# VectorE adds a chunk's window sums one step later, and GpSimd waits for seven gathers ahead of the eighth

## The chip, the cores and the metric

The kernel runs on one core of one Trainium2 chip. Its time is the device time of one execution in microseconds (us); where a kernel is timed, the median of its runs is given. The engines are TensorE (PE in the rows; its weight loads PEld), VectorE (DVE), ScalarE (ACT), GpSimd (POOL) and SyncE (SP). Each engine works through its own list of instructions in order, and they meet only through semaphores. DMAs are issued here by SP and by GpSimd.

## The reference, cut to what matters

A graph-attention layer over 6250 nodes and 200000 edges, and after it a layer of experts. The change lies in the edges of the first.

```python
h_fwd = h @ W_forward.T
h_rev = h @ W_reverse.T
messages = h_fwd[src] * direction[:, 0:1] + h_rev[src] * direction[:, 1:2]   # 200000 x 64
scores = leaky_relu(einsum('ef,hf->eh', messages, attn), 0.2)                # 4 heads
exp_scores = exp(scores - scores.max(axis=0))
sum_exp = segment_sum(exp_scores, dst)
norm = exp_scores / (sum_exp[dst] + 1e-10)
outs = [segment_sum(messages * norm[:, hd:hd + 1], dst) for hd in range(4)]
```

## The kernel before

First a table with one row of 136 numbers for each node is made (both products and their scores). Then comes the edge loop, which is what the change touches: the edges, sorted by destination, are taken in 98 chunks of 2048 (16 sets of 128). The loop is written with two chunks in its body, one for each of the two halves of the row buffer `rows` (`RING` = 2, slot `s`); the first two and the last four chunks are written out beside it. After it the nodes are normalised and routed, and the experts run.

A chunk's table rows come in two ways. Fourteen sets of 128 rows (`KG`) are gathered by GpSimd, one indirect DMA each (line 262). Two sets (`FILL`) are made without a DMA: VectorE builds two 0/1 matrices from the source numbers (`build_hot`, line 1043, tile `onehot`), TensorE multiplies each with the table that it holds in SBUF (`fetch`, line 966, 28 matmuls into `p_hot`), and VectorE picks the row out of seven candidates (`keep`, lines 1053 and 1058). The last two chunks gather all of their sets.

In step c VectorE does the following: it weighs the rows with the edges' weights (lines 990, 993, 996), makes the 0/1 matrix of destinations `hot` (1002), scores and their running maximum (1008, 1010, 1015), the messages `msg` (1019), and `hot_ex`, the destinations times the exponentials from ScalarE (1023). Then it keeps the two sets of chunk c+1 that TensorE has fetched, builds the first 0/1 matrix of chunk c+2, adds chunk c's eight windows of sums from PSUM into the accumulator (`finish`, line 985, tile `shared`), and builds the second 0/1 matrix of chunk c+2. In step c TensorE fetches the second set of chunk c+1, sums chunk c's messages into the eight windows (`sum_units`, line 878, tile `p_win`, semaphore `summed`), and fetches the first set of chunk c+2.

GpSimd runs ahead by one chunk. For chunk c it waits ahead of the first gather for the messages of chunk c-2 (whose buffer half it fills), ahead of the second for the sums of chunk c-2 (`summed`), ahead of the eighth for the scores of chunk c-1, and ahead of the twelfth for the messages of chunk c-1. `settle` is an increment that has nobody waiting for it. Each gather counts 16 on `gathered[s]` when it has landed; VectorE waits for the whole count of the chunk at the start of step c (`all_rows`). SP loads each chunk's indices with its edge weights, and the source numbers `key` for the 0/1 matrices, each repeated for all partitions.

Of the kernel before, what the change touches and what calls it, by code (L numbers as in the profile page):

```python
# [51 lines left out]
NCH = -(-EDGES // (CHUNK * RING)) * RING  # L52
# [10 lines left out]
KG = K - FILL  # L63
# [38 lines left out]
def after(eng, sem, count):  # L102

    if isinstance(count, int) and count <= 0:
        return
    eng.wait_ge(sem, count)


def settle(eng, turns):


    eng.sem_inc(turns, 1)
# [107 lines left out]
def stage_edges(nc, tensors, g):  # L220
# [4 lines left out]
    with ExitStack() as edges:  # L225
# [30 lines left out]
        gathered = [esem(f"gathered{s}") for s in range(RING)]  # L256
        prepared = esem("edges_prepared")

        def gather(pool, s, ks, done):

            for k in ks:
                pool.indirect_dma_start(out=rows[:, s, k, :], out_offset=None, in_=table,  # L262
                                        in_offset=bass.IndirectOffsetOnAxis(ap=index[:, s, 0, k:k + 1], axis=0))\
                    .then_inc(done, 16)
# [514 lines left out]
        with ExitStack() as ctx:  # L779
# [23 lines left out]
            msg_ready = sem("messages_ready")  # L803
# [5 lines left out]
            summed = sem("window_summed")  # L809
# [7 lines left out]
            def chunks(eng, begin, step, begun=0):  # L817


                loaded = begin(0)  # L820
                for s in range(begun, RING):
                    step(s, s, 0, loaded)
                with eng.Fori(1, NIT - 2) as it:
                    loaded = begin(it)
                    for s in range(RING):
                        step(it * RING + s, s, it, loaded)
                for it in range(NIT - 2, NIT):
                    loaded = begin(it)
                    for s in range(RING):
                        step(it * RING + s, s, it, loaded)  # L830

            def final(c):

                return isinstance(c, int) and c == NCH - 1
# [5 lines left out]
            def whole(it):  # L840

                return isinstance(it, int) and it == NIT - 1
# [9 lines left out]
            def fill_of(s, it):  # L852

                return (it - 1) * HOT + s * FILL

            def coming(s, it, ahead, j):


                t, jt = (s + ahead) % RING, it + (s + ahead) // RING
                if isinstance(jt, int) and not 0 < jt < NIT - 1:  # L860
                    return None
                return fill_of(t, jt) + j, t, jt, j
# [35 lines left out]
            @block.gpsimd  # L898
            def _(pool):
                def step(c, s, it, _):  # L900
                    pool.wait_ge(index_ready[s], 16 * (it + 1))
                    after(pool, msg_ready, c - RING + 1)
                    settle(pool, turns)
                    begun = EARLY_SETS if isinstance(c, int) and c == EARLY else 0
                    sets = K_LAST if final(c) else K if whole(it) else KG

                    def piece(a, b):
                        gather(pool, s, range(max(a, begun), min(b, sets)), gathered[s])

                    piece(0, 1)  # L910
                    after(pool, summed, c - 1)
                    settle(pool, turns)
                    piece(1, 7)
                    pool.wait_ge(score_ready, c)
                    settle(pool, turns)
                    piece(7, 11)
                    pool.wait_ge(msg_ready, c)
                    settle(pool, turns)
                    piece(11, K)
                pool.wait_ge(prepared, 1)  # L920
                chunks(pool, lambda it: None, step, EARLY)
# [53 lines left out]
            def _(dve):  # L975
# [11 lines left out]
                def step(c, s, it, loaded):  # L987
                    all_rows(dve, c, s, it)
                    attr_of = index[:, s, 1:3, :].bitcast(F32)
                    dve.tensor_tensor(rows[:, s, :, 0:COLS], rows[:, s, :, 0:COLS],  # L990
                                      attr_of[:, 0, :].unsqueeze(2).broadcast_to([P, K, COLS]), ALU.mult)\
                       .then_inc(fwd_part, 1)
                    dve.tensor_tensor(p_part[:, :, :], rows[:, s, :, COLS:COLS + HD],  # L993
                                      attr_of[:, 1, :].unsqueeze(2).broadcast_to([P, K, HD]), ALU.mult)\
                       .then_inc(rev_part, 1)
                    dve.tensor_tensor(rev_p, rows[:, s, :, COLS + HD:ROW],
                                      attr_of[:, 1, :].unsqueeze(2).broadcast_to([P, K, HEADS]), ALU.mult)\
                       .then_inc(rev_score, 1)
                    if isinstance(c, int) and c == 0:
                        dve.wait_ge(s_iota, 1)  # L1000
                    after(dve, val_ready, c)
                    dve.tensor_tensor(hot[:, :, :],
                                      dst_rel[:, ds(c * K, K)].unsqueeze(2).broadcast_to([P, K, W]),
                                      iota_p.unsqueeze(1).broadcast_to([P, K, W]), ALU.is_equal)\
                       .then_inc(hot_ready, 1)
                    dve.wait_ge(fwd_part, c + 1)
                    dve.wait_ge(rev_score, c + 1)
                    dve.tensor_tensor(raw[:, :, :], rows[:, s, :, HD:COLS], rev_p, ALU.add).then_inc(raw_ready, 1)
                    dve.wait_ge(raw_ready, c + 1)
                    dve.scalar_tensor_tensor(out=score[:, :, :], in0=raw[:, :, :], scalar=0.2, in1=raw[:, :, :],  # L1010
                                             op0=ALU.mult, op1=ALU.max).then_inc(score_ready, 1)
                    dve.wait_ge(score_ready, c + 1)
                    after(dve, max_taken, c)
                    real = K_LAST if final(c) else K
                    dve.tensor_tensor(run_max[:, 0:real, :], run_max[:, 0:real, :], score[:, 0:real, :], ALU.max)\
                       .then_inc(max_taken, 1)
                    dve.wait_ge(rev_part, c + 1)
                    after(dve, summed, c)
                    dve.tensor_tensor(msg[:, :, 0:HD], rows[:, s, :, 0:HD], p_part[:, :, :], ALU.add)\  # L1019
                       .then_inc(msg_ready, 1)  # L1020
                    dve.wait_ge(hot_ready, c + 1)
                    dve.wait_ge(exp_ready, c + 1)
                    dve.tensor_tensor(  # L1023
                        hot_ex[:, :, :, :],
                        hot[:, :, :].unsqueeze(2).broadcast_to([P, K, HEADS, W]),
                        ex[:, :, :].unsqueeze(3).broadcast_to([P, K, HEADS, W]), ALU.mult)\
                       .then_inc(val_ready, 1)
                    extra_windows(c, s, loaded[s])
                    if coming(s, it, 1, 0):
                        keep(*coming(s, it, 1, 0))  # L1030
                    if coming(s, it, 1, 1):
                        keep(*coming(s, it, 1, 1))
                    if coming(s, it, 2, 0):
                        build_hot(*coming(s, it, 2, 0))
                    finish(c)
                    if coming(s, it, 2, 1):
                        build_hot(*coming(s, it, 2, 1))

                def build_hot(f, s, it, j):

                    dve.wait_ge(key_ready[s], 16 * it)
                    after(dve, hot_rows, f - FILL + 1)
                    dve.tensor_tensor(onehot[:, j, :, :],  # L1043
                                      key[:, s, j, :].unsqueeze(1).broadcast_to([P, GP, P]),
                                      group_p.unsqueeze(2).broadcast_to([P, GP, P]), ALU.is_equal)\
                       .then_inc(hot_built, 1)
# [14 lines left out]
                def finish(c):  # L1061

                    words = load_own(dve, firsts[:, ds(c * UPC, UPC)], NP - 1)
                    dve.wait_ge(summed, c + 1)
                    for u in range(UPC):
                        after(dve, added, c * UPC + u)
                        add_window(p_win[0:MSG, u * HEADS * W:(u + 1) * HEADS * W], words[u])\
                            .then_inc(added, 1)
# [40 lines left out]
                dve.wait_ge(zeroed, 1)  # L1109
                dve.wait_ge(x_zeroed, NPART)  # L1110
                chunks(dve, begin, step)


def stage_nodes(nc, tensors, g):
# [1080 lines left out]
```

## Time and profile before

| | |
|---|---|
| median of 3 timed runs | 2554.95 us (2554.32 to 2557.01) |
| span of the profiled execution | 2909.8 us |
| busy in that span: TensorE, VectorE, GpSimd, ScalarE | 2151.1, 1860.1, 1744.0, 350.5 us |

The page gives the profiled execution's span from its first to its last instruction, and no time of its own beside that; whatever lies around the span comes on top. The span is 354.9 us longer than the median of the timed runs. Durations in the rows are therefore those of one execution that is some 14% longer than those that were timed. "issue" as the releaser of a wait says that the engine waited for nothing that the profile shows, "remote" that the event has no instruction to it in the trace.

### The profile page before, as it was taken

What the parts mean: (1) busy time and instruction counts of PE and PEld (TensorE: products, weight loads), DVE (VectorE), ACT (ScalarE), POOL (GpSimd) and SP (SyncE); (2) the same over time, 40 slices, a digit from 0 to 9 for tenths busy, and PEclk for the clock granted to TensorE, in tenths of its full rate; (3) what the DMA queues carried; (4) which work ended last, traced back from release to release, by engine and by line L of the source; (5) the groups of instructions that cost most, each with busy time, mean ns of one, the idle gap of its engine ahead of it and who ended that gap; (6) DMA issues with size and microseconds to landing.
All of it is one profiled execution on the core that took longest, in us unless ns stands there. A gap on an engine that the chain in (4) does not pass through costs nothing.

```text
span 2909.8 us, 44243 instructions
## 1 busy us (share of the span) xinstructions
PE 2151.1 (74%) x11977; PEld 1813.9 (62%) x11978; DVE 1860.1 (64%) x4481; ACT 350.5 (12%) x936; POOL 1744.0 (60%) x1757
## 2 busy tenths in 40 slices
PE   6587877778877676877777776777763547999990
PEld 6466765666666565666666665566653446888880
DVE  6666666657666665666576666567664566666656
ACT  4000000000000000000000000000002433434444
POOL 6667666667666666666666666567663554333326
PEclk8698888878788898988798988889875558999995
DMA  5222222222222222222222222222224456656657
GB/s 185 54 53 56 50 50 50 52 51 53 50 51 48 50 53 53 50 51 51 50 50 55 53 53 50 49 50 56 50 46 126 136 184 186 205 193 194 198 166 266
DMA packets 176304, 256.65 MB, mean 88 GB/s; under 512 B 47078, under 2 KB 120999, under 8 KB 176004
## 3 DMA queue, kind: packets, MB, share of 16 engines
q0 software_dynamic: 53696, 121.60, 16.9%
q1 hardware_dynamic: 122564, 134.56, 15.2%
q8 instruction: 16, 0.26, 0.0%
q14 instruction: 28, 0.23, 0.0%
HBM read 218.11 MB, written 38.79 MB: 88 GB/s over the span
## 4 chain that ended last, share of the span: by engine, by line
PE 32%; DVE 26%; issue 17%; another core or an unknown queue 14%; DVEq 7%; DMA 2%; POOL 1%; ACT 1%; SPq 0%; ACTq 0%; POOLq 0%
PE p_hot L966 28%; DVE p_hot L1053 4%; DVE onehot L1043 3%; DVEq L1702 3%; DVE shared L985 2%; DVEq L869 2%; DVE p_part L993 2%; DVE hot_ex L1023 1%; PE p_y L1870 1%; DVE p_y L1925 1%; PE p_h L1860 1%; DVE rows L990 1%; PE p_win L878 1%; DVE second L1905 1%
## 5 line engine op out<-in xcount | busy, mean ns | idle before, releaser
L262 POOL DMA_INDIRECT rows<-node_table,index x1375 | 1411.7, 1027 | 742.4 <-issue 446.5
L966 PE MATMUL p_hot<-parts,onehot 128*128 128x476 f32 x5264 | 1379.7, 419 | 467.7 <-DVE onehot L1043 256.0
L966 PEld LDWEIGHTS p_hot<-parts,onehot 128*128 128x128 f32 x5264 | 1092.9, 210 | 725.3 <-issue 283.1
L1053 DVE SCALAR_TENSOR_TENSOR p_hot<-place_no,place_of_source,p_hot 128x476 f32<-128x476 f32 x376 | 250.7, 712 | 350.4 <-remote 291.3
L985 DVE TENSOR_TENSOR shared<-shared,p_win 65x64 f32 x784 | 170.9, 218 | 361.2 <-remote 258.7
L878 PE MATMUL p_win<-hot_ex,msg 128*65 128x64 f32 x3136 | 231.7, 237 | 75.5 <-DVE hot_ex L1023 58.4
L928 ACT ACTIVATE ex<-score,neg_shift 128x64 f32<-128x64 f32 x98 | 34.3, 350 | 2087.2 <-DVE score L1010 1824.7
L878 PEld LDWEIGHTS p_win<-hot_ex,msg 128*65 128x65 f32 x3136 | 226.2, 152 | 94.7 <-issue 86.4
L1711 POOL DMA_INDIRECT expert_rows<-ys,back x104 | 103.1, 992 | 269.3 <-DVE ys L1930 195.5
L1058 DVE TENSOR_REDUCE rows<-p_hot 128x136 f32<-128x952 f32 x188 | 216.0, 1149 | 6.5
L1860 PEld LDWEIGHTS p_h<-xt,shared 128*128 128x128 f32 x1664 | 198.1, 193 | 35.2 <-ACT xt L1802 29.8
L1860 PE MATMUL p_h<-xt,shared 128*128 128x128 f32 x1664 | 210.2, 280 | 9.8 <-ACT xt L1802 7.5
L1870 PE MATMUL p_y<-shared,hid_t 128*128 x832 | 199.2, 383 | 10.4 <-DVE hid_t L1897 9.8
L1043 DVE TENSOR_TENSOR onehot<-key,p_dve 128x896 fp32r<-128x896 f32 x188 | 202.4, 1077 | 0.0
L1870 PEld LDWEIGHTS p_y<-shared,hid_t 128*128 128x128 f32 x832 | 151.0, 192 | 27.9 <-issue 11.2
L1281 POOL DMA_INDIRECT dispatched<-xn,slot_i x98 | 100.7, 1027 | 95.0 <-issue 72.5
L990 DVE TENSOR_TENSOR rows<-rows,index 128x1088 f32<-128x1088 f32 x98 | 126.2, 1287 | 36.1 <-issue 18.1
L1897 DVE TENSOR_SCALAR hid_t<-p_h,shared 128x128 f32<-128x128 f32 x208 | 63.4, 347 | 124.8 <-PE p_y L1870 68.3
L1019 DVE TENSOR_TENSOR msg<-rows,p_part 128x1024 f32<-128x1024 f32 x98 | 119.0, 1214 | 3.1 <-issue 3.1
L1023 DVE TENSOR_TENSOR hot_ex<-hot,ex 128x1024 f32<-128x1024 bf16 x98 | 119.4, 1219 | 1.0 <-issue 0.5
L993 DVE TENSOR_TENSOR p_part<-rows,index 128x1024 f32<-128x1024 f32 x98 | 120.0, 1225 | 0.0
L1833 ACT ACTIVATE own<-xs,is_first 128x256 f32<-128x256 f32 x104 | 52.9, 508 | 207.3 <-DVE is_first L1908 189.9
(268 smaller groups left out, 1401.3 us busy)
## 6 DMA issues: line engine op xcount, KB each, us to landing
shared<-in_w SPq DMA_DIRECT2D x120, 512.0 KB
rows<-node_table,index POOLq DMA_INDIRECT x1375
xs<-dispatched SPq DMA_DIRECT2D x104, 129.5 KB
key<-hot_keys SPq DMA_DIRECT2D x94, 128.0 KB
shared<-expert_rows SPq DMA_DIRECT2D x12, 896.0 KB, 8.6
token_rows<-in_x SPq DMA_DIRECT2D x7, 896.0 KB
shared<-in_x SPq DMA_DIRECT2D x7, 768.0 KB
out<-shared SPq DMA_DIRECT2D x6, 896.0 KB, 7.5
```

Of the source, the lines that this page charges most:

```text
L262: pool.indirect_dma_start(out=rows[:, s, k, :], out_offset=None, in_=table, in_offset=bass.IndirectOffsetOnAxis(ap=index[:, s, 0, k:k + 1] ...
L878: last = pe.matmul(psum[0:MSG, u * HEADS * W:(u + 1) * HEADS * W], msg[:, k, :], weighted[:, k, :, :].rearrange("p h w -> p (h w)"), start ...
L966: last = pe.matmul(p_hot[:, j, d, 0:PLACES * COLS], onehot[:, j, gr, :], parts[:, gr:NT:GP, m, d * COLS:(d + 1) * COLS], start=(gr == 0 an ...
L985: return dve.tensor_tensor(to, to, psum.rearrange("p (h w) -> p h w", h=HEADS), ALU.add)
L990: dve.tensor_tensor(rows[:, s, :, 0:COLS], rows[:, s, :, 0:COLS], attr_of[:, 0, :].unsqueeze(2).broadcast_to([P, K, COLS]), ALU.mult)\
L993: dve.tensor_tensor(p_part[:, :, :], rows[:, s, :, COLS:COLS + HD], attr_of[:, 1, :].unsqueeze(2).broadcast_to([P, K, HD]), ALU.mult)\
L1023: dve.tensor_tensor(hot_ex[:, :, :, :], hot[:, :, :].unsqueeze(2).broadcast_to([P, K, HEADS, W]), ex[:, :, :].unsqueeze(3).broadcast_to([P ...
L1043: dve.tensor_tensor(onehot[:, j, :, :], key[:, s, j, :].unsqueeze(1).broadcast_to([P, GP, P]), group_p.unsqueeze(2).broadcast_to([P, GP, P ...
L1053: last = dve.scalar_tensor_tensor(out=found[:, d], in0=place_no[:, :].unsqueeze(2).broadcast_to([P, PLACES, COLS]), scalar=place[:, ds(f, ...
L1058: dve.tensor_reduce(rows[:, s, KG + j, :].rearrange("p (d c) -> p d c", d=2), found.rearrange("p d v c -> p d c v"), AX.X, ALU.add).then_i ...
L1860: last = pe.matmul(p_h[:, u, f // 2, (f % 2) * P:(f % 2 + 1) * P], w1_r[:, r % R5, c, f * P:(f + 1) * P], xt[:, u, c, :], start=(c == 0), ...
L1870: last = pe.matmul(p_y[:, u, 0:D], hid_t[:, u, c, :], w2_sb[:, ds(e, 1), c, :] .rearrange("p a d -> p (a d)"), start=(c == 0), stop=(c == ...
```

## The change

In VectorE's step the eight window adds (`finish`) of chunk c leave step c and come in step c+1, between the running maximum and the messages; the first 0/1 matrix of chunk c+2 is built ahead of them, in step c. The messages' own wait for `summed` falls away, because the adds that now stand ahead of them wait for the same sums. The last chunk's adds stand behind the loop. A wait for VectorE's own messages of the step before is put ahead of line 993. GpSimd waits ahead of a chunk's eighth gather until the chunk's first seven have landed (`not begun` leaves out chunk 1 alone, whose first eight are gathered ahead of the loop).

```diff
                     piece(1, 7)
+                    if not begun:
+                        pool.wait_ge(gathered[s], 16 * (KG * it + 7))
                     pool.wait_ge(score_ready, c)
                     settle(pool, turns)
                     piece(7, 11)
...
                        .then_inc(fwd_part, 1)
+                    after(dve, msg_ready, c)
                     dve.tensor_tensor(p_part[:, :, :], rows[:, s, :, COLS:COLS + HD],
...
                        .then_inc(max_taken, 1)
+                    if coming(s, it, 2, 0):
+                        build_hot(*coming(s, it, 2, 0))
+                    if not (isinstance(c, int) and c == 0):
+                        finish(c - 1)
                     dve.wait_ge(rev_part, c + 1)
-                    after(dve, summed, c)
                     dve.tensor_tensor(msg[:, :, 0:HD], rows[:, s, :, 0:HD], p_part[:, :, :], ALU.add)\
...
                         keep(*coming(s, it, 1, 1))
-                    if coming(s, it, 2, 0):
-                        build_hot(*coming(s, it, 2, 0))
-                    finish(c)
                     if coming(s, it, 2, 1):
                         build_hot(*coming(s, it, 2, 1))
...
                 chunks(dve, begin, step)
+                finish(NCH - 1)
```

On VectorE, in the loop's body of the kernel before, the end of a step reads as follows: the last pick (`rows<-p_hot`), the first 0/1 matrix, the loading of the eight window places (`firsts`), and the first of the eight adds.

```order
L1058 TENSOR_REDUCE rows<-p_hot 128x136 [waits one_hot_rows_kept]
L1041 ISA
L106 ISA [waits keys_loaded0]
L1043 TENSOR_TENSOR onehot<-key,p_dve 128x896 [waits one_hot_rows_summed]
L869 ISA
L869 TENSOR_LOAD firsts
L985 ISA [waits window_added,window_summed]
L985 TENSOR_TENSOR shared<-shared,p_win 65x4x16
```

In the changed kernel the same instructions stand in the middle of the step, behind the running maximum.

```order
L1018 TENSOR_TENSOR run_max<-run_max,score 128x64 [waits max_taken,score_ready]
L106 REGISTER_ALU [waits keys_loaded1]
L1046 TENSOR_TENSOR onehot<-key,p_dve 128x896 [waits one_hot_rows_summed]
L869 ISA
L869 TENSOR_LOAD firsts
L987 ISA [waits window_added,window_summed]
L987 TENSOR_TENSOR shared<-shared,p_win 65x4x16
```

What moved is the matrix and the adds, from behind the picks to ahead of the messages; the wait for the sums went with the adds and is now for those of the chunk before.

On GpSimd, in the loop's body of the kernel before, one chunk of the second buffer half is this row of gathers (`x5` is five in a row).

```order
L262 DMA rows<-node_table,index 128x136 [waits index_ready1,messages_ready]
L262 DMA rows<-node_table,index 128x136 [waits window_summed]
L262 DMA rows<-node_table,index 128x136 x5
L914 REGISTER_ALU
L262 DMA rows<-node_table,index 128x136 [waits score_ready]
L262 DMA rows<-node_table,index 128x136 x3
L262 DMA rows<-node_table,index 128x136 [waits messages_ready]
L262 DMA rows<-node_table,index 128x136 x2
```

In the changed kernel it is this one.

```order
L262 DMA rows<-node_table,index 128x136 [waits index_ready1,messages_ready]
L262 DMA rows<-node_table,index 128x136 [waits window_summed]
L262 DMA rows<-node_table,index 128x136 x5
L916 REGISTER_ALU [waits gathered1]
L262 DMA rows<-node_table,index 128x136 [waits score_ready]
L262 DMA rows<-node_table,index 128x136 x3
L262 DMA rows<-node_table,index 128x136 [waits messages_ready]
L262 DMA rows<-node_table,index 128x136 x2
```

No gather moved; one wait more stands between the seventh and the eighth, on the count that the gathers themselves raise by landing.

## Rows read from the trace of the kernel before

**Rows 1.** The page, busy time: the span and the number of instructions.

```profile
span 2909.8 us, 44243 instructions
```

**Rows 2.** Stretches: length, engines' busy time (instructions), granted TensorE clock, DMA share, GB/s.

```profile
0.00:62.00 62.00, 43.15 (x322) 40.27 (x323) 37.16 (x154) 27.85 (x63) 42.58 (x45) 0.96 0.66 208
62.00:2213.00 2151.00, 1604.98 (x8408) 1322.71 (x8408) 1386.27 (x2435) 40.64 (x99) 1411.36 (x1375) 0.85 0.23 54
2213.00:2909.00 696.00, 502.98 (x3247) 450.91 (x3247) 436.66 (x1893) 281.97 (x774) 290.06 (x339) 0.80 0.56 182
```

**Rows 3.** The gathers' group: busy us, mean ns, then idle time before them by releaser.

```profile
L262 POOL DMA_INDIRECT rows<-node_table,index x1375 | 1411.7, 1027 | 742.4 <-issue 446.5 <-PE p_win L878 172.5 <-remote 104.6
```

**Rows 4.** Waits of VectorE and GpSimd in 62 to 2213: total us, times, longest.

```profile
DVE p_hot L1053 <- remote: 291.3, 29, 15.1
DVE shared L985 <- remote: 252.0, 71, 8.5
DVE rows L990 <- DMA rows<-node_table,index: 13.2, 1, 13.2
...
POOL rows L262 <- PE p_win L878: 172.5, 22, 11.7
POOL rows L262 <- remote: 104.6, 49, 2.8
POOL rows L262 <- DVE score L1010: 18.5, 8, 4.8
```

**Rows 5.** The stretch 1038.8 to 1053, columns as in rows 2.

```profile
1038.80:1053.00 14.20, 6.90 (x13) 3.46 (x14) 2.40 (x3) 0.26 (x1) 9.26 (x9) 0.67 0.29 60
```

**Rows 6.** Timeline around one step: start, length, instruction xcount [idle before it].

```profile
1103.40 6.37 PE L966 MATMUL p_hot<-parts,onehot 128*128 128x476 f32 x28 [1.40 <-DVE onehot L1043]
1103.56 1.29 DVE L990 TENSOR_TENSOR rows<-rows,index 128x1088 f32<-128x1088 f32 x1 [0.21 <-issue]
...
1108.15 1.22 DVE L1023 TENSOR_TENSOR hot_ex<-hot,ex 128x1024 f32<-128x1024 bf16 x1
1108.50 1.69 POOL L262 DMA_INDIRECT rows<-node_table,index  x1 [0.31 <-issue]
...
1109.61 2.10 PE L878 MATMUL p_win<-hot_ex,msg 128*65 128x64 f32 x32
...
1111.72 1.33 DVE L1053 SCALAR_TENSOR_TENSOR p_hot<-place_no,place_of_source,p_hot 128x476 f32<-128x476 f32 x2
...
1113.08 1.15 DVE L1058 TENSOR_REDUCE rows<-p_hot 128x136 f32<-128x952 f32 x1
1114.15 1.08 DVE L1043 TENSOR_TENSOR onehot<-key,p_dve 128x896 fp32r<-128x896 f32 x1
...
1115.28 6.59 PE L966 MATMUL p_hot<-parts,onehot 128*128 128x476 f32 x22 [3.57 <-DVE onehot L1043]
...
1117.05 2.66 DVE L985 TENSOR_TENSOR shared<-shared,p_win 65x64 f32 x8 [1.83 <-remote]
...
1120.63 1.28 DVE L990 TENSOR_TENSOR rows<-rows,index 128x1088 f32<-128x1088 f32 x1
```

**Rows 7.** Timeline around one blocked gather of GpSimd.

```profile
1009.66 0.94 POOL L262 DMA_INDIRECT rows<-node_table,index  x1 [0.30 <-issue]
1012.32 2.66 DVE L985 TENSOR_TENSOR shared<-shared,p_win 65x64 f32 x8 [3.05 <-remote]
1012.98 0.94 POOL L262 DMA_INDIRECT rows<-node_table,index  x1 [2.38 <-remote]
```

**Rows 8.** DMA issues: queue, count, KB each, median us from issue to landing.

```profile
key<-hot_keys SPq DMA_DIRECT2D x94, 128.0 KB
...
expert_rows<-ys,back POOLq DMA_INDIRECT x104, 2.5
...
attn_sb<-in_attn_t SPq DMA_DIRECT2D x1, 1.0 KB, 1.9
```

## The prediction

> **What bounds the kernel now.** I read the stretches first [rows 1, 2]: 62 us ahead of the edge loop, 2151 us in it, 696 us behind it. All edits lie in the loop. Then I read what the profiled execution is worth: its span of 2909.8 us is 354.9 us above the timed median of 2554.95 us, so it holds waits that a timed execution cannot have, and a step priced at one of them is priced wrongly. The waits view shows where they may be [rows 4]: VectorE's first pick waits 29 times, 291.3 us in all, about 10 us each, for a fetch. In one such stretch [rows 5] TensorE does 13 matmuls in 14.2 us, more than 1 us each, where 28 take 6.37 us [rows 6]; the granted share of 0.67 lies between the levels of 1.2 and 2.4 GHz and alone explains a factor of 2 at most. So TensorE sat still there, off and on, and 29 such stalls would be most of the excess. That a timed execution has few of them is inferred from the two totals, not seen.
>
> The third reading decides. GpSimd's gathers are busy 1411.4 us [rows 2], 1375 of them, each with a gap of 0.30 us to the next even where nothing blocks (the [0.30 <-issue] in rows 7). The loop cannot be shorter for GpSimd than 1411 + 1375 x 0.30 = 1824 us. The loop had 2151 us, so GpSimd waited 327 us in it, which the rows name: 172.5 and 104.6 us for the sums, 18.5 us for the scores, the rest under "issue" [rows 3, 4]. Take all these waits away and the execution is 2909.8 - 327 = 2583 us; the timed ones take 2555 us, even 28 us less. Unless the gathers are quicker without the profiler, **a timed execution has no waits left on GpSimd, and the gathers bound the loop**, at about 1824/98 = 18.6 us a chunk by the rows and (2555 - 758)/98 = 18.3 us by the timed total, where 758 = 62 + 696.
>
> The others are shorter. VectorE's step from one line 990 to the next is 1120.63 - 1103.56 = 17.07 us with a wait of 1.83 us in it [rows 6], so 15.2 us of work. TensorE has two fetches of 6.37 us and sums of 2.10 us, 14.8 us. The loop of dependences that runs through both before the change, first matrix 1.08, two fetches 12.74, last pick 1.33 + 1.15, is 16.3 us, or about 18 where the fetch starts at the lower clock (22 of its matmuls took 6.59 us after 3.57 us of idling, rows 6, where 28 take 6.37). So this loop is the runner-up, close behind.
>
> **The change part by part.** *Adds one step later.* The same 8 adds of 2.66 us together and the same loading of their places; no instruction is added on VectorE but the wait ahead of line 993, for messages that VectorE itself made a step ago: nothing. What goes is the adds' wait for the sums, 252.0 us in 71 waits [rows 4], 3.5 us each: a step later the sums have long been there. Is it on the path? In the profiled execution partly. By the reading above, in a timed one VectorE has 18.3 - 15.2 = 3 us a chunk to spare, so the wait costs nothing there, and its end gains nothing: what is late next is the gather. The queue behind it moves too: the messages, and with them `hot_ex`, TensorE's sums and GpSimd's twelfth gather, come 1.08 + 2.66 = 3.7 us later after the rows' arrival, at about 9 us instead of 5. GpSimd's twelfth gather of the next chunk starts some 14 us after that arrival, so it is not held.
>
> *First matrix ahead.* TensorE's first fetch needs the matrix and the first pick; the matrix is now there 10 us earlier, so TensorE starts after the first pick, 2.5 us after `hot_ex`, not after both picks and the matrix, 6 us. TensorE's list gets no longer. The loop of dependences through the last pick is cut, and TensorE's own 14.8 us and VectorE's 15.2 us remain. Worth 1 to 3 us a chunk if that loop bounded; behind the gathers it is worth 0, for the cover is the 18.3 us of GpSimd. SP's `key` loads wait for the second matrices, which stay.
>
> *The last chunk.* The adds of the last but one now stand ahead of the last messages: 2.66 us once, +3 us.
>
> *The wait on GpSimd.* It stands in 96 of 98 chunks (not in chunk 0, gathered ahead of the loop, nor in chunk 1). Behind it are queued the last seven gathers of the chunk and all later ones, and VectorE's step waits for them. At the wait the seventh gather has just been issued, so its whole flight is waited for. The trace has no time to landing for these gathers; the nearest row is GpSimd's other indirect DMA, 2.5 us [rows 8], larger and towards DRAM; the smallest transfer of the DMA list, 1 KB by SP, still takes 1.9 us. The next gather then starts later than the event by what a blocked one shows: VectorE's add and GpSimd's gather were released by the same sums, and the gather began 1012.98 - 1012.32 = 0.66 us after the add [rows 7]. Without the wait it would start 0.94 + 0.30 = 1.25 us after the seventh. So the price a chunk is between 1.9 + 0.66 - 1.25 = 1.31 us and, if the 2.5 us count from the end of the 0.95 us of issue, 2.86 us. Below that it is nothing where GpSimd would stand at this place anyway, which it did for 18.5 us in all [rows 4]. I take 2.5 us from the start, the same queue and kind: 1.91 us x 96 = **183 us**.
>
> The Trainium skill (DMA: Bandwidth & Descriptors, Anatomy of one DMA) puts a DMA issued by GpSimd at about 2.0 us and its bytes over 436 GB/s, an estimate of 2.16 us for these 69.6 KB; by that the price would be 151 us and the time 2709 us. No row here shows it.
>
> *Sum.* 2555 + 183 + 3 + 0 + 0 = **2741 us**, made from the profiled execution's durations on the timed median: the profiled span less GpSimd's waits is 2583 us, 28 us (1.1%) from that median, and the sum is uncertain by at least as much.
>
> **The rivals.** *GpSimd has slack in timed executions* (faster). If a gather's pitch without the profiler is well under 1.25 us, the 18.3 us a chunk are the loop through matrix, fetches and pick, and both of VectorE's edits pay. It decides below a pitch p at which 14 p + 1.1 (the mean of 1027 ns [rows 3] less the 0.95 of an undisturbed gather, 14 times) + 1.91 is under 18.3, so p = 1.09 us. With the 0.30 us gap hidden, p = 0.95, GpSimd's chunk is 16.3 us, VectorE's 15.2, and up to 2 us x 98 = 196 us go; half of that gives 2460 us. For it: the 252 us of waits and the matrix's place in the chain. Against it: the two totals, which fit the pitch of 1.25 within 1.1%. *A tie:* p near 1.09, gain and wait cancel, 2555 us, no change.
>
> *The wait takes time that was lost anyway.* A gather beside `hot_ex` takes 1.69 us, not 0.95 [rows 6]; over the loop such delays are 1375 x (1.027 - 0.95) = 106 us. If GpSimd now stands still where it was being held up, all of that is saved at best: 2741 - 106 = 2635 us. Against it: the wait comes at one place of the chunk and the delays are at several. The Trainium skill (SBUF, Who interferes with whom) says that a VectorE instruction with two SBUF inputs locks out a GpSimd one that reads SBUF; the trace agrees where it can, with that 1.69 us beside a 1.22 us `hot_ex`.
>
> *The wait is dearer.* The seventh gather shares the DMA engines with SP's 128 KB of `key` a chunk [rows 8], and the one wait for landed rows that the trace has was 13.2 us [rows 4]. At the upper price, 2.86 x 96 = 275 us: 2833 us.
>
> *The wait does not wait:* if GpSimd still stood at this place for the scores until the rows had landed, it would be free. That needs GpSimd to be early, so it is the tie or the faster case again.
>
> **How the numbers follow.** The forecast with its own range, 2690 to 2790: 0.58. Held-up time saved, or half a slack (2560 to 2690): 0.13. Dearer, to 2835: 0.06. The tie: 0.06. Faster, around 2460: 0.17. The range that leaves out the faster case and the far end of the dear one is 2550 to 2800 us, 0.8. A measurement of this kernel can tell 0.2% (5 us) from no change, so faster 0.17, same 0.06, slower 0.77.
>
> **What would show it.** Right: GpSimd's gathers get a new releaser, the DMA of the gathers themselves, about 96 times and 1.3 to 2 us each; VectorE's adds lose their "remote" wait; line 990 waits for the gathers in many chunks, not once; TensorE's fetch waits less for the matrix. Wrong: the new waits are there but the time falls, which says that GpSimd had slack; or they are short, which says that rows land sooner than 1.9 us; or the gathers' mean falls from 1027 ns towards 950, which is the held-up time. If the profiled span falls while the timed median rises, the adds' wait belonged to the profiled execution alone.

## The result, and the profile after

The changed kernel takes 2700.76 us (median of 4, 2697.99 to 2701.63) beside 2555.24 us for the kernel before (2554.32 to 2557.01): a ratio of 1.0566, 95% interval 1.0552 to 1.0581, or 145.5 us more. The forecast was slower by 186 us.

The page of the changed kernel: span, chain of work by engine, and the groups that answer to [rows 1, 3, 4] (busy us, mean ns of one | idle before them, its main releaser).

```profile
span 2696.2 us, 44146 instructions
...
POOL 34%; issue 26%; DVE 15%; DMA 12%; PE 7%; DVEq 5%; ACT 1%; SPq 1%; POOLq 0%; ACTq 0%
...
L262 POOL DMA_INDIRECT rows<-node_table,index x1375 | 1325.5, 964 | 651.9 <-issue 408.9
L968 PE MATMUL p_hot<-parts,onehot 128*128 128x476 f32 x5264 | 1221.6, 393 | 0.8 <-DVE rows L1061 0.8
...
L987 DVE TENSOR_TENSOR shared<-shared,p_win 65x64 f32 x784 | 170.3, 217 | 96.9 <-PE p_win L878 3.9
```

The profiled execution now agrees with the timed ones, as that of before did not [rows 1]. VectorE's adds have lost their wait for the sums (3.9 us against the 252.0 us in [rows 4]), and TensorE's fetches wait 0.8 us in all. Neither made the kernel faster. GpSimd's line has changed in two ways that pull against each other: its idle time is long and has a new cause, and its busy time is 86.2 us shorter than in [rows 3] for the same 1375 gathers.

The waits of GpSimd and VectorE in the changed kernel's loop, 62 to 2010: total us, times, longest.

```profile
POOL rows L262 <- issue: 403.4, 1242, 2.8
POOL rows L262 <- DMA rows<-node_table,index: 234.8, 95, 6.2
POOL rows L262 <- PE p_win L878: 5.8, 19, 0.3
...
DVE rows L992 <- DMA rows<-node_table,index: 460.6, 95, 7.7
```

GpSimd waits for its own gathers once a chunk, about 2.47 us, of which 0.30 is the gap that every gather has. VectorE in turn waits for landed rows in nearly every chunk: the engines behind the gathers have time to spare. One step of the changed kernel, as a timeline (start, length, instruction xcount [idle before it]):

```profile
1008.13 0.94 POOL L262 DMA_INDIRECT rows<-node_table,index  x1 [0.30 <-issue]
1008.32 1.29 DVE L992 TENSOR_TENSOR rows<-rows,index 128x1088 f32<-128x1088 f32 x1 [4.44 <-DMA rows<-node_table,index]
...
1011.86 1.09 DVE L1046 TENSOR_TENSOR onehot<-key,p_dve 128x896 fp32r<-128x896 f32 x1
...
1012.86 2.65 DVE L987 TENSOR_TENSOR shared<-shared,p_win 65x64 f32 x8
...
1014.50 0.94 POOL L262 DMA_INDIRECT rows<-node_table,index  x1 [0.30 <-issue]
...
1016.56 1.22 DVE L1029 TENSOR_TENSOR hot_ex<-hot,ex 128x1024 f32<-128x1024 bf16 x1
...
1017.93 0.94 POOL L262 DMA_INDIRECT rows<-node_table,index  x1 [2.49 <-DMA rows<-node_table,index]
```

The matrix and the adds stand where the change put them, ahead of the messages, so that `hot_ex` now comes 8.2 us after the rows. By then GpSimd stands still between its seventh gather (ends 1015.44) and its eighth (1017.93). In [rows 6] `hot_ex` fell on a gather and that one took 1.69 us; here nothing runs beside it.

So the theory to be tested was: the loop is bound by GpSimd's gathers, the wait costs its full price, and about a third of that comes back because `hot_ex` has been moved under it. The rivals: VectorE's new order pays for the difference; or the wait is simply cheaper than forecast; or the gathers' busy time in [rows 3] was long only because that execution was an odd one.

### The profile page after: what moved, and what is told of

It is laid out like the page before. It is cut to its first block, busy times and chain, and to the rows that moved or that the text cites. A ratio compares the mean times of both kernels' runs of the same rounds, so it can differ in the third digit from the quotient of the medians.

```text
span 2696.2 us, 44146 instructions
## 1 busy us (share of the span) xinstructions
PE 2090.1 (78%) x11977; PEld 1835.1 (68%) x11978; DVE 1854.0 (69%) x4481; ACT 349.0 (13%) x936; POOL 1657.0 (61%) x1757
## 4 chain that ended last, share of the span: by engine, by line
POOL 34%; issue 26%; DVE 15%; DMA 12%; PE 7%; DVEq 5%; ACT 1%; SPq 1%; POOLq 0%; ACTq 0%
POOL rows L262 33%; DMA rows<-node_table,index 10%; DVEq L1706 3%; PE p_win L878 3%; DVE p_y L1929 1%; DVE shared L987 1%; PE p_y L1874 1%; DVE hot_ex L1029 1%; DVE p_part L996 1%; PE p_h L1864 1%; DVE second L1909 1%; DVE hid_t L1901 1%; DVE back L1914 1%; DMA out<-shared 1%; DVE first_w L1922 1%
## 5 line engine op out<-in xcount | busy, mean ns | idle before, releaser
L262 POOL DMA_INDIRECT rows<-node_table,index x1375 | 1325.5, 964 | 651.9 <-issue 408.9
L968 PE MATMUL p_hot<-parts,onehot 128*128 128x476 f32 x5264 | 1221.6, 393 | 0.8 <-DVE rows L1061 0.8
L968 PEld LDWEIGHTS p_hot<-parts,onehot 128*128 128x128 f32 x5264 | 1029.3, 197 | 160.6 <-issue 0.7
L878 PE MATMUL p_win<-hot_ex,msg 128*65 128x64 f32 x3136 | 335.4, 298 | 426.8 <-DVE hot_ex L1029 426.8
L878 PEld LDWEIGHTS p_win<-hot_ex,msg 128*65 128x65 f32 x3136 | 319.0, 211 | 464.8 <-issue 464.8
```

The lines of the kernel that those rows point to most:

```text
L878: last = pe.matmul(psum[0:MSG, u * HEADS * W:(u + 1) * HEADS * W], msg[:, k, :], weighted[:, k, :, :].rearrange("p h w -> p (h w)"), start ...
L968: last = pe.matmul(p_hot[:, j, d, 0:PLACES * COLS], onehot[:, j, gr, :], parts[:, gr:NT:GP, m, d * COLS:(d + 1) * COLS], start=(gr == 0 an ...
```

## The experiments

Each kernel was timed in 4 or 5 runs beside the kernel before on the same chip (7 or 8 runs, median 2550.55 to 2552.13 us), but for the kernel before itself, of which one more execution was profiled.

**The kernel before, profiled again.** No edit.

> The kernel before, unchanged, profiled once more. Theory: the 355 us by which its first profiled span exceeded the timed runs, with TensorE's stalls and late sums, belong to that one profiled execution; a second may have a span near 2550 us, GpSimd idle for its gaps alone, a gather mean near 1010 to 1030 ns, and hot_ex beside gathers of 1.6 us. Rival: the excess belongs to this order of VectorE's work under the profiler, since the changed kernel and all variants with it had none but the variants with the old order had none either: again 2900 us.

It took 2560.11 us. Its page with the chain of work by engine, and below it the waits in 62 to 1900:

```profile
span 2558.4 us, 44243 instructions
...
PE 30%; DVE 20%; issue 18%; POOL 18%; DMA 6%; DVEq 6%; SPq 2%; ACT 1%; POOLq 0%; ACTq 0%
...
L262 POOL DMA_INDIRECT rows<-node_table,index x1375 | 1392.6, 1013 | 443.8 <-issue 430.3
...
L990 DVE TENSOR_TENSOR rows<-rows,index 128x1088 f32<-128x1088 f32 x98 | 126.7, 1293 | 337.3 <-DMA rows<-node_table,index 336.4
```

```profile
DVE rows L990 <- DMA rows<-node_table,index: 336.4, 97, 14.0
...
PE p_hot L966 <- DVE onehot L1043: 267.6, 93, 3.6
...
POOL rows L262 <- PE p_win L878: 13.1, 43, 0.3
DVE shared L985 <- PE p_win L878: 10.7, 3, 4.0
```

The 355 us that the first profile had too much are gone, and with them the 291.3 and 252.0 us of waits in [rows 4]. GpSimd has 443.8 us of idle time, of which 1375 x 0.30 = 412 are the gaps between gathers; VectorE waits for rows 97 times in 98 chunks. The gathers bound the loop of the kernel before. The chain of work seems to say otherwise, with 30% on TensorE and 18% on GpSimd. But where a gather follows an event of TensorE (43 times), it comes no later than 0.3 us, which is the gap that it has anyway: GpSimd loses nothing by it. The loop of dependences through TensorE and VectorE is close behind, and it is tried below by making the gathers fewer. This profile is the one to compare with: against it the changed kernel's gathers are 1392.6 - 1325.5 = 67.1 us less busy and 651.9 - 443.8 = 208.1 us more idle. The sum, 141.0 us, is the whole difference between the kernels but for 4.5 us; it has to be nearly that, since GpSimd does nothing else in the loop. What it tells is the split. Of the 86 us above, 19 belonged to the odd execution.

**The wait alone** (in the kernel before), and **the new order alone** (the changed kernel without the wait).

```diff
                     piece(1, 7)
+                    if not begun:
+                        pool.wait_ge(gathered[s], 16 * (KG * it + 7))
```

> The kernel before with GpSimd's new wait alone, VectorE's order as before. Theory: the gathers bound the loop, the wait costs 2.1 us in each of 96 chunks (200 us, as the changed kernel's idle time before its eighth gather), and the 86 us that the changed kernel's gathers became shorter (mean 1027 to 964 ns) came from the wait lying over hot_ex, where the new order puts it. In the old order hot_ex comes 3.7 us earlier and the wait does not cover it, so nothing is saved: about 2755 us, gather mean near 1020 ns. Rival one, VectorE's order plays no part and the wait itself spares the gathers: 2700 us, mean near 964 ns. Rival two, VectorE's new order is what costs: near 2555 us.

> The changed kernel without GpSimd's new wait: VectorE's new order alone. Theory: hidden behind the gathers, 2545 to 2570 us, gather mean between 1000 and 1030 ns, GpSimd idle only for its 0.30 us gaps in most places. Rival one, GpSimd had slack in timed runs and the loop of matrix, fetches and pick bounded: 2360 to 2500 us. Rival two, the adds ahead of the messages hold up GpSimd's twelfth gather or TensorE: 2600 us or more, with GpSimd waiting for messages.

The wait alone: 2756.03 us, ratio 1.0808 (1.0790 to 1.0826), +205.5 us. The order alone: 2539.68 us, ratio 0.9958 (0.9943 to 0.9972), -10.9 us. Added up, they give +195, which is 49 us more than both together. So the two parts are not independent. The gathers' groups of the wait alone and then of the order alone:

```profile
L262 POOL DMA_INDIRECT rows<-node_table,index x1375 | 1389.9, 1011 | 650.0 <-issue 413.9
```

```profile
L262 POOL DMA_INDIRECT rows<-node_table,index x1375 | 1380.1, 1004 | 443.6 <-issue 423.5
```

The wait alone brings the same idle time as in the changed kernel (650.0 against 651.9), but the gathers stay at 1011 ns. The order alone removes no idle time, only 12.5 us of busy time. Of these three kernels, only the one with both parts gets to 964 ns. The timeline of the wait alone shows why:

```profile
1002.05 1.22 DVE L1025 TENSOR_TENSOR hot_ex<-hot,ex 128x1024 f32<-128x1024 bf16 x1
1002.40 1.69 POOL L262 DMA_INDIRECT rows<-node_table,index  x1 [0.30 <-issue]
...
1004.39 0.94 POOL L262 DMA_INDIRECT rows<-node_table,index  x1 [0.30 <-issue]
...
1007.74 0.94 POOL L262 DMA_INDIRECT rows<-node_table,index  x1 [2.40 <-DMA rows<-node_table,index]
```

In the old order `hot_ex` is over before GpSimd comes to its wait, and still holds up a gather, here the sixth.

**The wait elsewhere:** the changed kernel with the wait ahead of the fourth gather.

```diff
-                    piece(1, 7)
-                    if not begun:
-                        pool.wait_ge(gathered[s], 16 * (KG * it + 7))
+                    piece(1, 3)
+                    if not begun:
+                        pool.wait_ge(gathered[s], 16 * (KG * it + 3))
+                        settle(pool, turns)
+                    piece(3, 7)
```

> The changed kernel with the wait moved from the eighth to the fourth gather (until the first three have landed). Theory: one flight is waited for as before (200 us), but the wait no longer lies over hot_ex, which again holds up a gather by 0.7 us in each chunk: 2760 us, gather mean 1000 ns or more. Rival, the place of the wait is of no account: 2700 us, mean near 964 ns.

It took 2771.88 us, ratio 1.0863 (1.0845 to 1.0882): with the same edits on VectorE and a wait of the same kind, 71 us more than the changed kernel (76 us, each against its own runs of before). Its group and a piece of its timeline:

```profile
L262 POOL DMA_INDIRECT rows<-node_table,index x1375 | 1401.9, 1020 | 653.1 <-issue 411.8
```

```profile
1010.72 0.94 POOL L262 DMA_INDIRECT rows<-node_table,index  x1 [2.38 <-DMA rows<-node_table,index]
...
1014.46 2.05 POOL L262 DMA_INDIRECT rows<-node_table,index  x1 [0.30 <-issue]
1014.47 1.22 DVE L1031 TENSOR_TENSOR hot_ex<-hot,ex 128x1024 f32<-128x1024 bf16 x1
```

The idle time is that of the changed kernel within 1.2 us, while the seventh gather takes 2.05 us. It is the wait's place beside `hot_ex` that gives time back: VectorE's order by itself, the same in both, doesn't, and nor does the wait at the eighth gather in the old order.

The timelines of the whole loop let the hold-ups be counted: gathers that end 0.80 to 0.84 us after a `hot_ex` (see the last section), and by how much they exceed the usual 0.945 us.

| kernel | held up by `hot_ex` | excess, us |
|---|---|---|
| before, second profile | 96 | 73 |
| wait alone | 96 | 73 |
| order alone | 97 | 61 |
| changed | 14 | 9.5 |
| changed, wait at the fourth | 92 | 88 |

From before to the changed kernel 64 of the 67.1 us of busy time are hold-ups by `hot_ex`. The order alone saves its 12 us (73 - 61) by hold-ups that are shorter, not fewer.

**The suspect taken away:** `ex`, one of the two operands of `hot_ex`, moved from SBUF into a free piece of a PSUM tile, in the kernel before and, without the wait, in the new order (there VectorE also waits for the exponentials ahead of the first matrix, which reads the same tile).

```diff
-            ex = sb("ex", [P, K, HEADS])
             p_dve = ps("p_dve", [P, 512])
+            ex = p_dve[:, 128:128 + K * HEADS].rearrange("p (k h) -> p k h", k=K)
```

> The kernel before with the exponentials (tile ex) in PSUM in place of SBUF, nothing else: ScalarE writes them there, VectorE's hot_ex reads one operand from SBUF and one from PSUM. Theory: a gather is held up by a VectorE instruction with two SBUF inputs, hot_ex the longest of them at 0.74 us a chunk; with one of them in PSUM that delay goes and the bounded loop with it, 71 us: about 2485 us, and the gathers beside hot_ex take 0.95 us. Rival one, the delay comes of something else that hot_ex does (its 16-bit operand, its write): 2555 us and 1.69 us beside hot_ex. Rival two, the gathers do not bound: 2555 us, though the gathers are shorter.

> VectorE's new order without GpSimd's new wait, and the exponentials in PSUM as in the run before it (VectorE waits for them ahead of the first 0/1 matrix, since both lie in one PSUM bank). Theory: both savings add, since each takes time off GpSimd's gathers alone: the new order alone brought 11 us, the exponentials in PSUM 70 us, together 2470 us, gather mean near 955 ns. Rival: with the gathers at their floor of 14 x 1.25 us a chunk another chain bounds, and the new order adds its own 25 us or more below that, or the wait for ScalarE costs: 2445 us or less, or 2490 us or more.

In the kernel before: 2480.20 us, ratio 0.9726 (0.9710 to 0.9743). In the new order: 2480.43 us, ratio 0.9727 (0.9711 to 0.9743). **Moving one tile makes this 70 us faster than the kernel before, and some 216 us faster than the changed one (each against its own runs of before).** The group and a piece of the timeline of the former:

```profile
L262 POOL DMA_INDIRECT rows<-node_table,index x1375 | 1317.3, 958 | 443.5 <-issue 434.4
```

```profile
1003.18 1.21 DVE L1023 TENSOR_TENSOR hot_ex<-hot,p_dve 128x1024 f32<-128x1024 bf16 x1
1003.53 0.94 POOL L262 DMA_INDIRECT rows<-node_table,index  x1 [0.30 <-issue]
```

Beside the same instruction of the same length, a gather takes 0.94 us. The gathers' busy time falls by 75.3 us and the time by 70. The new order brings nothing on top: without hold-ups both kernels stand at the gathers' own pitch, and the expectation of 10 us more was wrong. With that the 11 us of the order alone are also explained by busy time (12.5 us), not by VectorE.

**Another bound:** two of the fourteen gathers left out in most chunks, in the old order and in the new one, both without the wait.

> The kernel before with two of a chunk's fourteen gathers left out in chunks 2 to 95 (their rows keep what the chunk before left there, so the sums are other ones; everything else is done). Theory: GpSimd's chunk falls by 2 x 1.25 us to about 16 us, 235 us over 94 chunks; in the old order the loop of first matrix, two fetches and last pick takes 16.3 us at full clock and up to 18 us with cold starts, so it now bounds and part of the saving is lost: 2350 to 2480 us, with GpSimd waiting. Rival, nothing but the gathers matters: 2315 us.

> VectorE's new order without GpSimd's new wait, with the same two gathers left out. Theory: that loop is cut, TensorE's 14.8 and VectorE's 15.2 us lie under GpSimd's 16 us, so the whole saving arrives: 2540 - 235 = 2305 us, at least 30 us below the run with the old order, which is what VectorE's new order is worth once the gathers are out of the way. Rival, the new order is worth nothing even then: the same time as the old order with twelve gathers.

Old order 2396.27 us, ratio 0.9395 (0.9379 to 0.9412); new order 2277.22 us, ratio 0.8926 (0.8911 to 0.8940). The chain of the old order by engine, and its waits in 200 to 1700:

```profile
PE 57%; DVE 19%; issue 9%; DVEq 8%; DMA 3%; POOL 2%; SPq 1%; ACT 1%; ACTq 0%; POOLq 0%
```

```profile
PE p_hot L969 <- DVE onehot L1046: 160.4, 88, 1.8
DVE p_hot L1056 <- PE p_hot L969: 148.1, 88, 2.5
POOL rows L263 <- PE p_win L881: 77.1, 62, 1.7
```

The chain of the new order, and its waits in the same stretch:

```profile
POOL 38%; issue 30%; DVE 13%; PE 7%; DVEq 5%; DMA 4%; SPq 1%; ACT 1%; POOLq 0%; ACTq 0%
```

```profile
DVE rows L993 <- DMA rows<-node_table,index: 59.3, 91, 14.4
```

In the old order the loop of dependences, matrix to fetch to pick, has taken over from the gathers: TensorE waits for VectorE's matrix and VectorE for TensorE's fetch, 88 times each. The new order cuts it, the chain is back on GpSimd, and 119 us are gained. So VectorE's edit does what it says and is worth 119 us here, where it is the bound, and 11 us where the gathers are. GpSimd's waits for the sums (77.1 us) fell away too. The new order's time lies 28 us below what was expected of it. Some 20 of them are pauses of GpSimd (last section), 1.9 us each beyond the gap: the loop of the order alone has 12, this one has one.

**The price of the wait by itself:** with `ex` in PSUM, so that there is nothing to give back, one wait in the old order, two waits in the old order (the second ahead of the fourth gather, as above), and one wait in the new order.

> The old order of VectorE with `ex` in PSUM (no gather is held up by `hot_ex`) and the wait ahead of the eighth gather. Theory: the wait costs its full price, 206 us of GpSimd's idle time as in the run of the wait alone (650.0 - 443.8), and nothing is given back, since nothing is held up any more: 2480 + 206 = 2686 us, between 2675 and 2695, with the gathers' mean at 0.96 us. Rival: the 86 us that the gathers' busy time lost in the changed kernel have nothing to do with `hot_ex`; then the wait costs some 145 us here too, 2625 us.

> The kernel of the run before with a second wait, ahead of the fourth gather, for the first three. Theory: the price is per wait, paid by GpSimd at any place of the chunk: 2480 + 2 x 206 = 2892 us, between 2870 and 2910, two waits of 2.4 us per chunk. Rival: what the wait costs is a queue of transfers behind the seven gathers, which a first wait has drained already; then the second is cheaper, under 2850 us.

> The changed kernel with `ex` in PSUM (VectorE waits for the scores' exponentials ahead of the first matrix, as in the earlier run with that buffer). Theory: the changed kernel has already got back nearly all of the held-up time, so PSUM brings it only the 14 collisions that are left, some 10 us: 2690 us, between 2682 and 2698, equal to the old order with the wait and `ex` in PSUM within 10 us. Rival: what was given back comes from the order and adds to what PSUM gives, 75 us: 2625 us.

2685.24 us (ratio 1.0527, 1.0509 to 1.0544), 2890.59 us (1.1335, 1.1316 to 1.1354) and 2686.21 us (1.0524, 1.0506 to 1.0541). All three came within 4 us of the theory and 40 us or more from the rivals. The gathers' groups, one kernel each in this order:

```profile
L262 POOL DMA_INDIRECT rows<-node_table,index x1375 | 1316.9, 958 | 651.0 <-issue 414.1
```

```profile
L262 POOL DMA_INDIRECT rows<-node_table,index x1375 | 1314.0, 956 | 858.2 <-DMA rows<-node_table,index 473.2
```

```profile
L262 POOL DMA_INDIRECT rows<-node_table,index x1375 | 1318.2, 959 | 650.6 <-issue 410.7
```

One wait costs 2685.24 - 2480.20 = 205.0 us, a second one 205.4 us more: 2.1 us a chunk, at either place, in either order. The changed kernel with `ex` in PSUM is only 14.6 us faster than without (11.4, each against its own runs of before), where the kernel before gains 70: most of what PSUM would give, the wait's place had already given.

**Busy and idle time of one group.** For each kernel whose gathers are whole: how much the busy and idle time of line 262 together differ from those of the second profile of before (1392.6 + 443.8 = 1836.4 us), beside the measured difference of the medians.

| kernel | busy + idle of line 262, us | less 1836.4 | measured |
|---|---|---|---|
| changed | 1325.5 + 651.9 | +141.0 | +145.5 |
| wait alone | 1389.9 + 650.0 | +203.5 | +205.5 |
| order alone | 1380.1 + 443.6 | -12.7 | -10.9 |
| changed, wait at the fourth | 1401.9 + 653.1 | +218.6 | +221.3 |
| `ex` in PSUM | 1317.3 + 443.5 | -75.6 | -70.4 |
| order alone, `ex` in PSUM | 1317.0 + 443.6 | -75.8 | -70.4 |
| `ex` in PSUM, one wait | 1316.9 + 651.0 | +131.5 | +133.1 |
| `ex` in PSUM, two waits | 1314.0 + 858.2 | +335.8 | +338.5 |
| changed, `ex` in PSUM | 1318.2 + 650.6 | +132.4 | +134.1 |

That the columns agree within 5.4 us shows that all differences arise in the loop, and whether as busy or as idle time. It doesn't show what bounds the loop: line 262 is all that GpSimd does there, so its busy and idle time are the loop's length whatever bounds it. The old order with twelve gathers fits as well (1221.0 + 458.3 is 157.1 less, measured 154.5), and there the gathers don't bound. That they do in the kernels of the table is shown by what the idle time consists of (gaps, the added waits and the pauses, and hardly another wait), and by `ex` in PSUM, which shortens the gathers and little else and brings 70 us.

## Why the prediction was right, and what was mis-sized

- **The gathers bound a timed execution:** right. It was inferred from two totals, against the waits of the profile at hand; the second profile of before shows it (VectorE waits for rows 97 times, no gather waits for another engine beyond its gap), and so does `ex` in PSUM. Of the 28 us by which the forecast's sum of gathers missed the timed median, 19 were longer gathers of the odd execution.
- **The profiled execution's excess:** right that it belonged to that execution, and that the adds' 252.0 us were no gain to be had. Why that one ran 355 us long is open.
- **VectorE's edits are worth 0 behind the gathers:** nearly right. The order alone gave 10.9 us, but as gathers less held up, not as a shorter path. The reason that was given, a loop of dependences hidden behind GpSimd, is shown by the kernels with twelve gathers: uncovered, the edit is worth 119 us, and that loop takes about 17.1 us a chunk (1221.0 + 458.3 us over 98 chunks), between the forecast's 16.3 and 18.
- **`hot_ex` 9 us after the rows instead of 5, and GpSimd's twelfth gather not held by it:** right; 8.2 us (1008.32 to 1016.56; the forecast's rows give 4.6 + 3.7 = 8.3), and no wait for messages in GpSimd's list.
- **The last chunk, +3 us:** not measured by itself; it is too small to be told.
- **The wait, 1.91 us x 96 = 183 us:** too small by 22; alone it costs 205 us. The seventh and the eighth gather start 1017.93 - 1014.50 = 3.43 us apart in the timeline above, where the forecast had 2.5 + 0.66 = 3.16. The difference is in the flight: it was taken from another transfer's 2.5 us, and the changed kernel's list of DMA issues (queue, count, median us to landing) has the one that was missing in [rows 8]:

```profile
rows<-node_table,index POOLq DMA_INDIRECT x1375, 2.8
```

- **Held-up time:** the step that failed. It was a rival with a bound of 106 us, set against the forecast, and put aside because "the wait comes at one place of the chunk and the delays are at several". They are mostly at one: taking away `hot_ex`'s second SBUF operand alone brings the gathers' mean from 1013 to 958 ns, (1.013 - 0.958) x 1375 = 76 us. And the forecast had itself worked out that `hot_ex` would come 4 us later. It asked of that only whether GpSimd's twelfth gather would wait, not which gather would run beside `hot_ex` then. The answer is hardly any (14 in 98 chunks, after 96), because of the wait. So this was no rival but one more term: 183 + 22 - 67 + 3 = 141 us instead of 186; measured 145.5. That sum was made after the fact. The two errors have opposite signs, which was luck: with the wait at its measured price and the rest as it was, the forecast would have been 208 us.

The Trainium skill (SBUF — State Buffer, Who interferes with whom) has the rule behind that term, that a VectorE instruction with two SBUF inputs contends with a GpSimd instruction that reads SBUF, and that one with at most one, outside VectorE's two-port modes, does not. The runs with `ex` in PSUM agree: 958 ns a gather instead of 1013, in the kernel before with nothing else changed.

## What to carry to other kernels

Where one engine's list of equal instructions bounds a loop, add up its busy and idle time and ask of every edit, those on other engines too, what it does to either; a wait that the edit removes elsewhere is worth nothing while the other engines stay shorter. That busy and idle time add up to the loop's length proves nothing about the bound; look at what the idle time consists of. When an edit moves an instruction that is known to disturb the bounding engine, work out what stands beside it at its new place, as a term of the sum. And when a profiled execution is far longer than the timed ones, profile it again before any of its waits is priced.

## What the runs showed of the hardware

- **A gather is held up by where it starts, not by how far it overlaps.** One that starts with `hot_ex` (both inputs in SBUF) or while it runs ends 0.82 us after `hot_ex` does, whether it started early or late in it: 1002.40 + 1.69 against 1002.05 + 1.22 with the wait alone, and 1014.46 + 2.05 against 1014.47 + 1.22 with the wait at the fourth. One that had started 0.19 us before such an instruction keeps its 0.94 us: the one at 1008.13 in the changed kernel, beside line 992 from 1008.32. In the seven profiles from kernels with `ex` in SBUF (the second one of the kernel before, not the odd one) 588 gathers were held up so, the earliest starting 0.05 us before `hot_ex`, the latest 1.05 us after its start. Those that started in its last 0.2 us kept their 0.94 us, by which they end later anyway. Two that started 0.01 us after it weren't held; there `hot_ex` took 0.05 us longer than usual. With one input in PSUM `hot_ex` holds up none (180 gathers ran beside it in the kernel before with `ex` in PSUM).
- **Waiting for an indirect gather to land costs 2.1 us of GpSimd's time** beyond the gap that is there anyway, at both places that were tried: some 2.4 us of idling instead of 0.30.
- **Left open:** in every eighth chunk (each 112 gathers) GpSimd pauses for some 2.2 us ahead of the second gather with nothing to wait for that the profile shows, 12 times in the loop of the changed kernel as in the others. With twelve gathers a chunk it does so once. No run looked for the cause. The changed kernel's timeline has this one:

```profile
1029.80 1.56 POOL L262 DMA_INDIRECT rows<-node_table,index  x1 [2.19 <-issue]
```
